# A fused attention block: x transposed by 16 transfers and VectorE instead of TensorE, three groups ahead

## What is computed

```python
xn = layernorm(x, g_in)                       # (x - mean) * rsqrt(var + 1e-5) * g
q = (xn @ Wq).reshape(b, n, H, DH).transpose(0, 2, 1, 3) * DH ** -0.5
k, v = split(xn @ Wkv)                        # one head of 64 each
k = concatenate([null_k, k]); v = concatenate([null_v, v])
sim = einsum('bhid,bjd->bhij', q, k) + concatenate([null_bias, attn_bias])
sim = where(causal_mask, neg, sim)            # query i sees keys 0..i and the null key
sim = where(mask, sim, neg)
out = einsum('bhij,bjd->bhid', softmax(sim), v) @ Wo
return x + layernorm(out, g_out)
```

## Time and profile before

| | us |
|---|---|
| runs | 1154.99, 1156.02, 1156.12; median 1156.02 |
| profiled execution, first to last instruction | 1154.5 |
| TensorE busy | 1061.4 |
| POOL busy | 804.2 |
| VectorE busy | 729.0 |
| ScalarE busy | 674.2 |

### The profile page before, as it was taken

One profiled execution on the slowest core, in us unless ns is written; L12 is line 12 of the kernel. 1 busy time (PEld: TensorE's weight loads), 2 busy tenths in 40 slices (PEclk: granted clock), 3 DMA queues, 4 the chain that ended last, 5 costly groups with the idle time before them and its releaser, 6 DMA issues.

```text
span 1154.5 us, 43028 instructions
## 1 busy us (share of the span) xinstructions
PE 1061.4 (92%) x14464; PEld 923.9 (80%) x14464; DVE 729.0 (63%) x3536; ACT 674.2 (58%) x2666; POOL 804.2 (70%) x1488
## 2 busy tenths in 40 slices
PE   4799999999999999999999999999999999999975
PEld 4678888888888888888888888888888888888864
DVE  4757666656666666766765766755766665666551
ACT  3656556566556556556655655656655656655651
POOL 2657777667777667777767777767777766777763
PEclk9999999999999999999999999999999999999987
DMA  8211211211221211220221121121121121121011
GB/s 224 64 40 49 67 57 40 66 61 45 68 65 31 67 60 47 66 67 31 65 66 44 65 66 41 55 66 56 50 68 51 45 67 58 48 66 47 30 39 36
DMA packets 51548, 67.72 MB, mean 59 GB/s; under 512 B 13888, under 2 KB 25664, under 8 KB 51392
## 3 DMA queue, kind: packets, MB, share of 16 engines
q1 hardware_dynamic: 49280, 63.21, 17.6%
q10 hardware_dynamic: 2112, 2.10, 0.6%
HBM read 40.11 MB, written 16.78 MB: 49 GB/s over the span
## 4 chain that ended last, share of the span: by engine, by line
PE 77%; ACT 8%; issue 6%; DVE 4%; POOL 1%; ACTq 0%; DVEq 0%; POOLq 0%
PE ps_pv L424 33%; PE ps_proj L430 32%; PE ps_s L387 7%; PE ps_pv L411 4%; ACT exp_bot L679 3%; ACT exp_top L679 2%; DVE o_lo L513 2%; ACT xt_hi L710 1%; DVE logit_bot L492 1%; PE ps_proj L448 1%; ACT o_hi L687 1%; ACTq L221 0%; DVEq L221 0%; DVE y_stats L521 0%; DVEq L225 0%
## 5 line engine op out<-in xcount | busy, mean ns | idle before, releaser
L679 ACT ACTIVATE exp_bot<-logit_bot,neg_max 128x129 f32<-128x129 f32 x512 | 201.7, 397 | 342.3 <-DVE neg_max L492 336.9
L430 PE MATMUL ps_proj<-xt_hi,wq_hi 128*128 128x256 f32 x1024 | 298.5, 292 | 4.1 <-DVE q_sb L568 3.9
L790 POOL TENSOR_TENSOR bias_b<-bias_c,mask_add 128x256 f32<-128x256 f32 (+1 forms) x512 | 289.6, 598 | 1.6 <-DVE neg_max L492 0.3
L492 DVE CUSTOM_DVE_ANT_0 logit_bot<-ps_s,bias_b 128x128 f32<-128x128 f32 x512 | 128.7, 289 | 255.4 <-PE ps_s L387 226.8
L430 PE MATMUL ps_proj<-xt_lo,wq_hi 128*128 128x256 f32 x1024 | 288.0, 281 | 0.0
L430 PE MATMUL ps_proj<-xt_hi,wq_lo 128*128 128x256 f32 x1024 | 287.9, 281 | 0.0
L424 PE MATMUL ps_pv<-wo_hi,o_hi 128*128 128x512 f32 x512 | 211.8, 414 | 51.1 <-DVE o_lo L513 51.1
L799 POOL TENSOR_TENSOR w_nrm<-exp_bot,w_inv 128x256 f32<-128x256 f32 x256 | 156.6, 612 | 120.0 <-DVE w_inv L501 118.8
L424 PE MATMUL ps_pv<-wo_lo,o_hi 128*128 128x512 f32 x512 | 204.9, 400 | 0.0
L424 PE MATMUL ps_pv<-wo_hi,o_lo 128*128 128x512 f32 x512 | 204.8, 400 | 0.0
L430 PEld LDWEIGHTS ps_proj<-xt_hi,wq_hi 128*128 128x128 f32 x1024 | 192.8, 188 | 14.3 <-issue 5.1
(11 more groups left out here) (61 smaller groups left out, 1850.7 us busy)
## 6 DMA issues: line engine op xcount, KB each, us to landing
x_in<-in_x_dram SPq DMA_DIRECT2D x32, 512.0 KB, 4.1
x_res<-in_x_dram SPq DMA_DIRECT2D x64, 256.0 KB, 2.8
out_dram<-y_out SPq DMA_DIRECT2D x64, 256.0 KB, 2.0
v_rep<-v_raw SPq DMA_DIRECT2D x256, 32.0 KB, 1.9
w_raw<-in_L_cond_Wq_dram ACTq DMA_DIRECT2D x4, 512.0 KB, 7.9
w_raw<-in_L_cond_Wo_dram SPq DMA_DIRECT2D x4, 512.0 KB, 6.1
mask_u<-in_mask_BxS_bk_dram SPq DMA_DIRECT2D x32, 32.0 KB, 3.7
bias_c<-in_fside_16xSxS_dram SPq DMA_DIRECT2D x4, 128.0 KB, 8.1
```

Source lines behind the costliest of these rows:

```text
L430: mm = pe.matmul(ps[:, 0:TOK], w[:, k, cols], xt[:, k], start=(j == 0), stop=(j == len(todo) - 1))
L492: ins = nc.vector.tensor_tensor_reduce(out_[:, e, 0:keys_], ps_s[e][:, from_:from_ + keys_], bias[:, e], -1.0, 0.0, ALU.add, ALU.min, neg_ ...
L679: ins = nc.scalar.activation(out_[:, s, j], in_[:, s, j], ACT.Exp, bias=neg_max[:, s, k:k + 1], scale=-1.0, accum_out=w_sum[:, s, k:k + 1])
L790: ins = nc.gpsimd.tensor_tensor(out_, bias, key_mask, ALU.add)
```

## The change

- g_in is multiplied into the weights Wq and Wkv when they are split, in pieces of 256 (Wkv 128) columns, instead of into xt.
- Groups 0 and 1 are still transposed by TensorE (`BY_PE = 2`). From group 2 on, ScalarE writes xn with its columns in an order by blocks of 32; SP moves it with 16 transfers of 32 partitions (`split_x`) into `x_split`, so that each 32x32 block lies in its final rows and columns; one block transpose on VectorE (`turned`, 128x1024) makes `x_turned` in SBUF; ScalarE copies xt_hi from it (`x_high`, two of 128x512) and VectorE subtracts (`x_low`, two of 128x512).
- x_in, xt_hi and xt_lo get two slots. Loads, statistics, scale and xn run three groups ahead: statistics and scale at step 3, xn at step 5; transfers after it; the block transpose and xt_hi at step 3 of the next group; xt_lo at its step 7.
- The key/value tile moves from step 2 to step 1, the Q tiles by one place: q6, q7 at step 0, kv at 1, q0 at 2, q1 and q2 at 4, q3 and q4 at 5, q5 at 6. ScalarE still takes keys and v from the bank at step 2.
- v is block-transposed at step 3 of the group that uses it, not at step 7 of the group before.
- SP's order is changed to fit, and the start: ScalarE's xn of group 0 comes before Wkv's high part, POOL's scale of group 1 before the causal fill of the bias.

```diff
@@ -47,22 +48,23 @@
 
 
 FRONT = {
-    0: [("q", 5, 0), ("q", 6, 0)],
-    1: [("q", 7, 0), ("x", 0, 1), ("x", 1, 1)],
-    2: [("kv", 0, 1)],
-    4: [("q", 0, 1), ("q", 1, 1)],
-    5: [("q", 2, 1), ("q", 3, 1)],
-    6: [("q", 4, 1)],
+    0: [("q", 6, 0), ("q", 7, 0)],
+    1: [("kv", 0, 1)],
+    2: [("q", 0, 1)],
+    4: [("q", 1, 1), ("q", 2, 1)],
+    5: [("q", 3, 1), ("q", 4, 1)],
+    6: [("q", 5, 1)],
 }
 FRONT_FIRST = FRONT | {
     0: [("q", 4, 0), ("q", 5, 0)],
     1: [("q", 6, 0), ("q", 7, 0), ("x", 0, 1), ("x", 1, 1)],
+    2: [("kv", 0, 1), ("q", 0, 1)],
 }
-PARTS = [("x", 0), ("x", 1), ("kv", 0)] + [("q", i) for i in range(QT)]
+PARTS = [("kv", 0)] + [("q", i) for i in range(QT)]
 USE = {part: j for j, part in enumerate(PARTS)}
 USES = len(PARTS)
-PROLOGUE = PARTS[:USE["q", 4]]
-STEP_STATS, STEP_XN, STEP_V, STEP_MASK = 4, 7, 7, 7
+PROLOGUE = [("x", 0), ("x", 1)] + PARTS[:USE["q", 4]]
+STEP_KV, STEP_STATS, STEP_TURN, STEP_XH, STEP_V, STEP_XN, STEP_XL, STEP_MASK = 2, 3, 3, 3, 3, 5, 7, 7
...
-        x_in = sb("x_in", [P, GB, DIM])
+        x_in = sb("x_in", [P, 2, GB, DIM])
...
+        x_split = sb("x_split", [P, GB, N // BLK, P])
+        x_turned = sb("x_turned", [P, KT, TOK])
+        xt_hi, xt_lo = sb("xt_hi", [P, 2, KT, TOK], F32R), sb("xt_lo", [P, 2, KT, TOK], F32R)
...
+        def run_pairs_ahead(eng, body):
+            body(0, True, True, False)
+            with eng.Fori(1, PAIRS - 2) as p:
+                body(p, False, True, False)
+            body(PAIRS - 2, False, False, False)
+            body(PAIRS - 1, False, False, True)
+
+        def three_ahead(p, t, loads, last):
+            if t // CG and loads:
+                yield 2 * p + 4, p + 2, 0
+            elif not (t // CG or last):
+                yield 2 * p + 3, p + 1, 1
...
+        def bank_of(slot, kind, i):
+            return ps_proj[(slot + (i if kind == "x" else USE[kind, i])) % 2]
+
+        def proj_count(f, kind, i):
+
+            before = USES * f + XT * (min(f, BY_PE - 1) + 1 if isinstance(f, int) else BY_PE)
+            return before - XT + i + 1 if kind == "x" else before + USE[kind, i] + 1
+
+        def halves_of(f, slot, i, from_pe):
+
+            k = slice(KX * i, KX * (i + 1))
+            if from_pe:
+                turned = bank_of(slot, "x", i)[:]
+            else:
+                turned = x_turned[:, k].rearrange("p k n -> p (k n)")
+            return turned, *(xt[:, slot, k].rearrange("p k n -> p (k n)") for xt in (xt_hi, xt_lo))
...
-                sp.wait_ge(xn_made, GB * (2 * q + k))
+                sp.wait_ge(xn_made, GB * (2 * q + k - 1))
...
+            def split_x(f):
+                wait(sp, xn_made, GB * (f + 1))
+                apart(sp)
+                wait(sp, x_turned_made, f - BY_PE)
+                apart(sp)
+                for a in range(N // BLK):
+                    for r in range(P // BLK):
+                        sp.dma_start(x_split[BLK * r:BLK * (r + 1), :, a],
+                                     xn[BLK * a:BLK * (a + 1), :, P * r:P * (r + 1)]).then_inc(ld_split, 16)
...
             def body(p, first, loads, last):
 
-                if not first:
+                if not last:
+                    load_x_and_mask(p + 1, 1)
+                if first:
+                    split_x(BY_PE)
+                else:
                     store(p, -2, True)
                 spread_v(2 * p + 1)
+                if not last:
+                    split_x(2 * p + 3)
                 if not first:
                     store(p, -1, True)
-                if not last:
-                    load_x_and_mask(p + 1, 1)
+                if loads:
+                    load_x_and_mask(p + 2, 0)
                 store(p, 0, True)
                 if not last:
                     spread_v(2 * p + 2)
+                if loads:
+                    split_x(2 * p + 4)
                 store(p, 1, True)
-                if loads:
-                    load_x_and_mask(p + 2, 0)
                 if last:
...
+                ps = bank_of(slot, kind, i)
+                by_pe = isinstance(f, int) and f < BY_PE
                 if kind == "x":
+                    wait(pe, q_made, QT * f - XT + i + 1)
                     if i == 0:
                         wait(pe, xn_made, GB * (f + 1))
                     for j in range(KX * GB):
                         k, b = KX * i + j // GB, j % GB
                         mm = pe.transpose(ps[:, N * j:N * (j + 1)], xn[:, b, P * k:P * (k + 1)], ident[:])
                 elif kind == "kv":
+                    if not by_pe:
+                        wait(pe, q_made, QT * f - 1)
                     wait(pe, xt_lo_made, XT * (f + 1))
-                    mm = project(ps, wkv_hi, wkv_lo, slice(0, 2 * DH))
+                    mm = project(ps, slot, wkv_hi, wkv_lo, slice(0, 2 * DH))
                 else:
+                    if i == 0 and not by_pe:
+                        wait(pe, q_made, QT * f)
+                    elif i == 1:
+                        wait(pe, v_raw_made, f + 1)
+                    elif i > 1:
+                        wait(pe, q_made, QT * f + i - 1)
                     if isinstance(f, int) and f == 0:
-                        wait(pe, wq_lo_made, i * WP // QT + 1)
-                    mm = project(ps, wq_hi, wq_lo, slice(P * i, P * (i + 1)))
+                        wait(pe, wq_lo_made, KT * (i * WP // QT + 1))
+                    mm = project(ps, slot, wq_hi, wq_lo, slice(P * i, P * (i + 1)))
...
+            def turned(f):
+
+                wait(dve, ld_split, 16 * SPLITS * (f - BY_PE + 1))
+                wait(dve, xt_lo_made, XT * f)
+                nc.vector.transpose(x_turned[:].rearrange("p k (a j) -> p a k j", j=BLK),
+                                    x_split[:].rearrange("p b a (k i) -> p (b a) k i", i=BLK)).then_inc(x_turned_made, 1)
+
+            def x_low(f, slot, i, from_pe):
+                x_raw, hi, lo = halves_of(f, slot, i, from_pe)
+                wait(dve, xt_hi_made, XT * f + i + 1)
+                nc.vector.tensor_tensor(lo, x_raw, hi.bitcast(F32), ALU.subtract).then_inc(xt_lo_made, 1)
...
+            dve.wait_ge(wkv_hi_made, KT)
+            for k in range(KT):
+                nc.vector.scalar_tensor_tensor(
+                    out=wkv_lo[:, k], in0=wkv_raw[:, 2 * DH * k:2 * DH * (k + 1)], scalar=gin_col[:, k:k + 1],
+                    in1=wkv_hi[:, k].bitcast(F32), op0=ALU.mult, op1=ALU.subtract).then_inc(wkv_lo_made, 1)
...
-                ("q", 1): lambda: (wq_low(2), x_stats_of(1), x_mean_var_of(1)),
+                ("q", 1): lambda: (x_stats_of(0, 1), x_mean_var_of(1), wq_low(2)),
...
-                            if t % CG == STEP_STATS:
-                                x_stats_of(2 * p + t // CG + 2)
-                            if t % CG == STEP_STATS + 1:
-                                x_mean_var_of(2 * p + t // CG + 2)
+                            if t % CG == STEP_TURN and not (first and t < CG):
+                                turned(2 * p + t // CG + 2)
                             if t % CG == STEP_MASK:
                                 mask_of(2 * p + t // CG + 2, t // CG)
-                        if t % CG == STEP_V and not (last and t > CG):
-                            spread_v_of(2 * p + t // CG + 1, (t // CG + 1) % 2)
+                            if first and t == STEP_XL:
+                                turned(BY_PE)
+                        if t % CG == STEP_STATS:
+                            for f, q, k in three_ahead(p, t, loads, last):
+                                x_stats_of(q, k)
+                                x_mean_var_of(f)
+                        if t % CG == STEP_V:
+                            spread_v_of(2 * p + t // CG, t // CG)
                         if t % 2:
                             inverse(n, t)
-
-            run_pairs(dve, body)
+                        if t % CG == STEP_XL and not last:
+                            for i in range(XT):
+                                x_low(2 * p + t // CG + 2, t // CG, i, False)
+
+            run_pairs_ahead(dve, body)
...
                                      scale=y_rstd[:, b:b + 1]).then_inc(y_nrm_made, 1)
 
-            def x_norm(f):
+            def x_norm(f, slot):
                 wait(act, x_shift_made, f + 1)
-                wait(act, proj_done, USES * (f - 1) + XT)
+                if isinstance(f, int) and 0 < f <= BY_PE:
+                    wait(act, proj_done, proj_count(f - 1, "x", XT - 1))
+                if not (isinstance(f, int) and f <= BY_PE):
+                    wait(act, ld_split, 16 * SPLITS * (f - BY_PE))
                 for b in range(GB):
-                    nc.scalar.activation(xn[:, b], x_in[:, b], ACT.Identity, bias=x_shift[:, b:b + 1],
+                    normed = xn[:, b].rearrange("p (r k i) -> p k r i", r=P // BLK, k=KT)
+                    if isinstance(f, int) and f < BY_PE:
```

(44 more changed lines are left out.)

93 lines of the change are left out of this document (38 added, 55 removed).

## The result

The kernel after takes 1105.34 us (median of 4 runs, 1102.51 to 1105.91) against 1155.51 us before: ratio 0.9568, 95% interval 0.9551 to 0.9584. Its profiled span is 1103.9 us, before 1154.5. The forecast was 1094.0, 11 us too low; the range and the sign held, the narrower own range of the forecast (1087 to 1101) did not.

The account below looks back on a forecast made before the run. TensorE, busy 1061.4 of 1154.5 us, was taken as the bound, with a wait before step 3's output projection. 1156.0 - 63 (30 groups at 2.1 us) + 1 (start) = 1094.0 us; range 1088 to 1123.

Parts of the forecast that it names:

- The loss before the change: Per steady group: transposes cost TensorE 1.27 us, and their copies' queue time led to 1.46 us idle before step 3's output projection.
- The gain of 2.1 us a group: Step 3's output projection comes 2.1 us earlier after the group's first scores; over 30 groups, 63 us.
- S + 9.93: Step 3's output projection, 9.93 us after the group's step 0 scores start (S); read from the last group, without x work.
- R4: Rival: both losses go, the transposes' time and the wait before step 3's output projection; 82 us gained, 1075 us; chance 0.03.
- kv, q7 and q0 at nothing: Key/value tile at step 1, q7 at step 0, q0 at step 2: no price; 0.5 us in the last group.
- Step 3 and xn at step 5: Work added on VectorE (3.9 to 4.0 us) and ScalarE (1.2 us; xn 1.52 us) fits into idle time; price 0.
- R2: Rival: a new wait, at xn in step 5 or VectorE's step 3, replaces the old one; 1119 us; chance 0.12.
- x_low at nothing: VectorE's two xt_lo subtractions at step 7 get in beside POOL; price taken 0, at most 0.9 us on step 0.
- R1: Rival: xt_lo is shut out until POOL's train ends, step 0 logits 0.9 us late; 1121 us; chance 0.19.
- Transfers: Sixteen more per group on SP, 0.62 us each, 10 us; SP's work 18 of 32 us; price 0.
- R3: Rival: SP's queue becomes the bound, slower from 1.65 us per issue; 1238 us at 1.82 us; chance 0.06.
- The start: Prologue with g_in put into the weights and POOL's scale of group 1 earlier: between -2 and +5 us, taken as +1.

Follow-up runs that it names:

- e3: Kernel before, without six of the eight TensorE transposes in groups 1 to 31 (values wrong): 1146.7 us, ratio 0.9904.
- e4: Kernel before, all transposes kept, without ScalarE's xt_hi and VectorE's xt_lo copies in groups 1 to 31 (values wrong): 1113.4 us, ratio 0.9639.
- e10: e5 plus POOL's mask additions of one step moved ahead of the scale of y: 1083.41 us, ratio 0.9369.
- e6: Kernel after, each of the sixteen transfers issued twice, the second into a spare tile: 1311.13 us, ratio 1.1353.
- e1: Kernel after, with xn of group 3 made at step 7 of group 0 instead of step 5: 1100.51 us, ratio 0.9524.
- e2: e1 plus statistics and scale of group 3 at step 7 of group 0 instead of step 3: 1099.75 us, ratio 0.9518.
- e8: e2 with VectorE's statistics of group 3 ahead of the block transpose of step 7 of group 0: 1099.85 us, ratio 0.9517.
- e7: e1 with Wq split whole without g_in (values wrong) and POOL's scale of group 1 behind the causal fill again: 1097.41 us, ratio 0.9495.
- e5: e1 with ScalarE's y_nrm behind the exponentials of the odd step instead of before them: 1099.93 us, ratio 0.952.

## Why the prediction was right, and where it was off

*The loss before the change* was read rightly as double. e3 and e4 put sizes on it: transposes alone 0.34 us a group, the copies behind them 1.24 us.

*The gain of 2.1 us a group* came as 2.06. S + 9.93 from the last group was a good yardstick, but the reason given, "the length of the ScalarE and VectorE chain without the x work", was half of it: POOL's chain ends at the same place. In the kernel before, too, w_nrm of step 0 ended at 1104.80 in that last group and exp_bot of step 2 began at 1104.96. Taking the time from a group that had lost the x work covered both chains without my knowing the second; that part was luck. R4's size (both losses go) was reached once both were shortened (e10), not by the change.

*kv, q7 and q0 at nothing*: right. TensorE's rows of the steady group show no wait but the one of 0.59 us. e3 shows what covering q7 was worth: 13.0 us when its cover goes.

*Step 3 and xn at step 5*: right, R2 did not come. Line groups of the kernel after (busy us, mean ns, then the idle time before, by releaser), which answer to the earlier trace rows:

```profile
L607 DVE TENSOR_TENSOR xt_lo<-x_turned,xt_hi 128x512 fp32r<-128x512 f32 x60 | 52.4, 913 | 0.6 <-ACT xt_hi L787 0.6
L776 ACT ACTIVATE xn<-x_in,small 128x512 f32<-128x512 f32 x64 | 48.4, 804 | 18.5 <-POOL small L903 10.9 <-DMA x_split<-xn 7.6
L601 DVE STREAM_TRANSPOSE x_turned<-x_split 128x1024 f32<-128x1024 f32 x30 | 36.3, 1210 | 0.0
```

The block transpose took 1.21 us (1.3 to 1.4 forecast) and never waited for its transfers; writing xn in pieces of 32 cost nothing (two in 1.51 us); the 7.6 us for x_split are the single wait of the start.

*x_low at nothing, R1*: right in its effect. It does contend. VectorE and POOL around it:

```profile
526.13 1.75 DVE L607 TENSOR_TENSOR xt_lo<-x_turned,xt_hi 128x512 fp32r<-128x512 f32 x2
530.83 0.29 DVE L546 CUSTOM_DVE_ANT_0 logit_bot<-ps_s,bias_b 128x128 f32<-128x128 f32 x1 [2.95 <-PE ps_s L439]
...
526.49 0.84 POOL L887 TENSOR_TENSOR w_nrm<-exp_top,w_inv 128x128 f32<-128x128 f32 x1
527.30 1.74 POOL L920 TENSOR_TENSOR y_nrm<-y_nrm,gout_row 128x512 f32<-128x512 f32 x1
529.11 1.27 POOL L924 TENSOR_TENSOR y_out<-y_nrm,x_res 128x512 f32<-128x512 f32 x1
```

The two take 1.75 us instead of 1.38, so they lose 0.37 us, and POOL's w_nrm and y_nrm take 0.84 and 1.74 instead of 0.40 and 1.30, so POOL loses 0.88 us. That is what turns at the ends of instructions would give, and both had slack (2.95 us before the logits). The Trainium skill (SBUF — State Buffer, Who interferes with whom) says that a VectorE instruction with two SBUF inputs contends with GpSimd's reads of SBUF, and, of VectorE's two-port modes, that whoever issues first gets the shared pair for the whole instruction. These rows agree with an exclusion of one instruction at a time. By that rule wo_lo in the earlier trace rows would not have stood for 4.58 us behind a whole train, and why it did is still open.

*Transfers*: 0.60 us an issue (0.62 taken), no wait in steady groups, R3 did not come. But the sum was short, and its point of decision was wrong. A train takes 11.8 us in the median, not 10, and SP's queue is taken for 19.8 us a group, not 18. And I took the time per group in which SP's queue is full, 1.65 us an issue. e6 doubles the issues, about 1.45 us per original transfer, and is already 13% slower than before: the loop through x_in, the statistics and SP's own order decides, not the sum. The price of nothing was right only with a margin much smaller than I thought.

*The start*: this is the step that failed. The prediction said "Between -2 and +5; I take +1"; it was +10.7. It priced the prologue and left out what the three-groups-ahead scheme adds in group 0: group 0 carries two xn, two statistics and two trains of transfers where later groups carry one. (Two xn stood in group 0 before as well, at 31.34 and 60.94; new is that the second must wait for a train.) Its cover of 0.3 us for xn was read from a steady group. 4.8 us are settled: xn of group 3 behind the transfers of group 2 (e1). Of the rest, the second set of statistics held the first output projection by 3.4 us, but little of it could be won back (e2, e8): 1.5 us went to the clock, and the transfers of group 3 are late as well. What is left over is in part the prologue (0 to 3 us, e7) and in part the clock. Granted clock in four windows of the kernel after (window, busy times, PEclk, DMA share, GB/s):

```profile
30.00:35.00 5.00, 4.49 (x46) 4.41 (x47) 1.20 (x11) 1.11 (x6) 4.85 (x11) 0.50 0.87 294
35.00:40.00 5.00, 5.00 (x39) 5.00 (x39) 2.11 (x13) 0.44 (x4) 2.49 (x5) 0.86 0.17 60
65.00:70.00 5.00, 0.91 (x2) 0.83 (x3) 1.93 (x6) 4.73 (x16) 0.76 (x2) 0.71 0.17 48
70.00:75.00 5.00, 5.00 (x15) 3.87 (x14) 3.95 (x9) 2.34 (x10) 2.46 (x4) 0.61 0.08 21
```

It was 1.00 in the first two before. TensorE had been busy for 1.66 of the 5 us ahead of them, before for 2.69. At 0.50, the lower level of 1.2 GHz, TensorE loses 2.5 of the 5 us and 0.7 of the next: up to 3.2 us, of which an unknown part was hidden. I did not separate this. The last two windows follow the wait of 6.96 us, and their price can be read: from the start of the first output projection to S of group 1 the same 24 matmuls take 7.96 us here, 5.78 in e1, where the wait is 1.69 us and the clock 1.00 from 60 to 75 us, and 7.33 before, where the wait is 2.89 us and the clock 0.68 from 60 to 65. So 2.2 us of what e1 won at S of group 1 is the clock, and against the kernel before the difference is 0.6 us of the 10.8.

## What to carry to other kernels

When a change makes work run further ahead, price the first turn of the loop by itself: it holds the work of several turns, and a cover read in a steady one says nothing about it; look for an instruction at the head of a queue that waits for transfers of a tile that an earlier one still reads. When a fix of the chain that "ends last" gives nothing, look for a second chain at the same instruction before giving it up; here two edits were worth 0 and 0 alone and 17 us together. Transfers can become the bound before their queue is full: in e6 their queue was taken for 29.4 us a group, less than the turn of 32.3 us, and a group took 39.2 us, because the loop that ran through the queue was longer than the turn.

## What the runs showed of the hardware that I had not expected

- A train of 16 transfers of 32 partitions within SBUF takes 10.4 to 13.5 us to issue, 11.8 in the median of 30, not 16 x 0.60 = 9.6: now and then one takes 1.4 us or more (407.47 in e6).
- A VectorE subtraction with both inputs in SBUF took 0.69 us alone and 0.91 in the mean beside POOL, and POOL's two instructions paid 0.44 us each in the group shown above. The wo_lo of 4.58 us before the change took 2.84 us in the kernel after, from 55.79: POOL's own wo_lo ran from 55.15 for 2.40 us, and VectorE's ended 1.08 us behind its end, as it had ended 1.08 us behind the end of the train before the change. POOL's next instruction was the same in both, a mask addition queued directly behind its wo_lo: after, it started at 57.50 and took 1.72 us, so VectorE went in ahead of it; before, it started at 48.53 and took 0.74 us, and VectorE stayed out. What decides this is not shown.
- The clock behind a wait: the first output projection ran its matmuls in 0.63 us each at a granted 0.61 and in 0.40 us at 1.00, and from its start to the next scores took 7.96 against 5.78 us (kernel after, e1). But a wait of 3.12 us in e5 was followed by 1.00, and one of 3.28 us in e2 by 0.71.
